# Scaling the gathered expert rows on ScalarE and adding them on VectorE eight tiles at a time

## The reference

```
out = x + attn(xn) + ffn(xn)
```

```
gates   = softmax(tokens @ Wg);  idx = argmax(gates);  kept = place < 1024
expert_out[e] = relu(expert_in[e] @ W1[e] + b1[e]) @ W2[e] + b2[e]
ffn[t]  = gates[t, idx] * kept * expert_out[idx][place of t]
```

## Time and profile before

| | us |
|---|---|
| median of three runs | 1358.07 (1357.27 to 1358.6) |
| the profiled execution: its span, from the first to the last instruction | 1358.0 |
| VectorE busy | 1248.0 (92%) |
| TensorE busy | 1012.7 (75%) |
| GpSimd busy | 930.7 (69%) |
| ScalarE busy | 749.5 (55%) |
| the 64 adds (L890), busy | 54.5 |
| the 64 gathers (L538), busy on GpSimd | 72.8 |

### The profile page before, as it was taken

The page is one execution under the profiler, slowest core; times in us unless marked ns, Lnnn a source line. Parts: engine busy times, 40 slices in busy tenths (PEclk is TensorE's granted clock), DMA queues, the critical chain, the costliest instruction groups (busy, mean ns, idle before and its releaser), DMA issues.

```text
span 1358.0 us, 15420 instructions
## 1 busy us (share of the span) xinstructions
PE 1012.7 (75%) x3725; PEld 468.5 (34%) x3725; DVE 1248.0 (92%) x1491; ACT 749.5 (55%) x1147; POOL 930.7 (69%) x737
## 2 busy tenths in 40 slices
PE   0867378888888888888788886776867677686675
PEld 0422134434344443434344442332322233232232
DVE  7689599898999979898999989999999999999997
ACT  2665247666566657666566655555555555555421
POOL 3248886677676757686677767686867768686655
PEclk9978579999899989999899999788988979898766
DMA  6512131211212121211212021111102121110211
GB/s 143 146 42 74 38 109 32 78 32 39 70 29 56 24 78 31 77 31 39 70 34 55 20 53 42 47 47 47 46 0 53 39 48 44 46 46 1 54 39 47
DMA packets 62895, 69.53 MB, mean 51 GB/s; under 512 B 11488, under 2 KB 49280, under 8 KB 62848
## 3 DMA queue, kind: packets, MB, share of 16 engines
q1 hardware_dynamic: 58752, 60.65, 18.0%
q0 software_dynamic: 4096, 8.40, 2.0%
HBM read 18.69 MB, written 16.78 MB: 26 GB/s over the span
## 4 chain that ended last, share of the span: by engine, by line
DVE 37%; issue 30%; PE 20%; POOL 5%; ACT 3%; SPq 2%; DVEq 2%; DMA 1%; POOLq 0%; ACTq 0%
DVE u_sb L899 14%; DVE s_sb L983 7%; PE bank L1185 3%; DVE sp_q L848 3%; POOL expert_in L567 3%; PE bank L1178 3%; PE bank L1203 3%; PE bank L1218 2%; DVE acc L890 2%; PE bank L1196 2%; PE bank L1144 2%; DVE g_sb L857 1%; PE bank L1161 1%; DVE dd L905 1%; DVE sp_l L851 1%
## 5 line engine op out<-in xcount | busy, mean ns | idle before, releaser
L560 POOL TENSOR_TENSOR s_sb<-s_sb,c_of 128x512 f32<-128x512 f32 x480 | 649.6, 1361 | 317.8 <-DVE s_sb L983 313.1
L983 DVE TENSOR_TENSOR_SCAN s_sb<-bank,u_sb 128x512 f32<-128x512 f32 x512 | 619.8, 1211 | 0.0
L739 ACT ACTIVATE bank<-bank,a_neg 128x510 f32<-128x510 f32 x512 | 337.2, 660 | 449.8 <-PE bank L1203 440.1
L1196 PE MATMUL bank<-dsp,sel_d 128*128 128x512 f32 x512 | 318.9, 623 | 102.0 <-DVE u_sb L899 91.0
L899 DVE TENSOR_TENSOR u_sb<-bank,b_of 128x512 f32<-128x512 f32 x512 | 345.4, 675 | 49.5 <-PE bank L1196 40.7
L1203 PE MATMUL bank<-dsp,sel_d 128*128 128x512 f32 x512 | 255.5, 499 | 117.0 <-DVE s_sb L983 110.4
L1196 PEld LDWEIGHTS bank<-dsp,sel_d 128*128 128x128 f32 x512 | 106.5, 208 | 305.4 <-DVE u_sb L899 238.5
L1203 PEld LDWEIGHTS bank<-dsp,sel_d 128*128 128x128 f32 x512 | 107.0, 209 | 262.9 <-DVE s_sb L983 241.7
L1218 PE MATMUL bank<-s_sb,con 128*32 128x512 f32 x1024 | 156.8, 688 | 28.1 <-POOL s_sb L560 24.2
L1129 PE MATMUL bank<-xnT,wx 128*128 (+1 forms) x256 | 133.1, 615 | 0.0
L567 POOL DMA_INDIRECT expert_in<-xn,put_at x64 | 68.1, 1065 | 22.2 <-issue 17.6
(11 more groups left out here) (134 smaller groups left out, 1117.2 us busy)
## 6 DMA issues: line engine op xcount, KB each, us to landing
dsp<-hi SPq DMA_DIRECT2D x64, 256.0 KB
dsp<-dd SPq DMA_DIRECT2D x64, 256.0 KB
expert_in<-dd SPq DMA_DIRECT2D x8, 512.0 KB, 6.2
xn<-expert_in SPq DMA_DIRECT2D x8, 512.0 KB, 4.2
xn<-L_ffn_W SPq DMA_DIRECT2D x16, 256.0 KB, 4.6
expert_out<-xn SPq DMA_DIRECT2D x16, 256.0 KB, 2.5
out<-acc SPq DMA_DIRECT2D x8, 512.0 KB, 5.2
expert_in<-xn,put_at POOLq DMA_INDIRECT x64, 2.2
```

The lines of the kernel that those rows point to most:

```text
L560: pool.tensor_tensor(s_now, s_now, c_of[:, hf, hh, :], ALU.mult).then_inc(S["p_ready"], 1)
L739: act.activation(d, d, ACT.Exp, scale=a_neg[:, k:k + 1]).then_inc(S["decay_ready"], 1)
L983: dve.tensor_tensor_scan(s_sb[:, w % S_RING, :], decay_of(w)[:, :], u_sb[:, w % U_RING, :], 0.0, ALU.mult, ALU.add).then_inc(S["scan_done" ...
L1196: pe.matmul(du_ps[w % 2][:, :], sel_d[:, group_of(w), :, :].rearrange("k n d -> k (n d)"), dsp[:, hf, head_of(w), 1, :], start=True, stop= ...
```

## The change

ScalarE multiplies the gathered rows by their gates, in place in `back`, one tile an instruction: two tiles in each of slots 10 to 13 (`SCALE` = 10, `SCALE_EACH` = 2), after the exponential of the slot and ahead of its other work. It waits for all eight gathers there. VectorE adds the whole group in one operation of 128x1024 in slot 16 and waits for the scaled tiles. The gates of a group are copied by VectorE to `gate_now`, next to the row numbers. For the last group, ScalarE scales all eight tiles after its last slot, and VectorE's add comes after the last gate and no longer before it.

```diff
-GATHER, COMBINE = 1, 14
+GATHER, SCALE, COMBINE = 1, 10, 16
+SCALE_EACH = 2
+        gate_now = sb("gate_now", [P, GROUP])
...
+            def scale_back(ch, tiles, extra=0):
+                act.wait_ge(S["back_loaded"], lin(ch, lambda c: 16 * GROUP * (c - FIRST_COMBINE + extra + 1)))
+                for n in tiles:
+                    act.activation(back[:, n, :], back[:, n, :], ACT.Copy, scale=gate_now[:, n:n + 1]
+                                   ).then_inc(S["back_scaled"], 1)
...
                     act.activation(d, d, ACT.Exp, scale=a_neg[:, k:k + 1]).then_inc(S["decay_ready"], 1)
+                    if has_combine(ch) and 0 <= w - SCALE < GROUP // SCALE_EACH:
+                        scale_back(ch, range((w - SCALE) * SCALE_EACH, (w - SCALE + 1) * SCALE_EACH))
...
-            chunks(act, body, lambda: None)
+            chunks(act, body, lambda: scale_back((CHUNKS - 1, None), range(GROUP), 1))
...
+                dve.tensor_copy(gate_now[:, :], gate[:, bass.ds(k, GROUP)])
                 dve.tensor_copy(take_now[:, :], take_at[:, bass.ds(k, GROUP)]).then_inc(S["take_ready"], 1)
...
-            def combine(ch, n, extra=0):
-                dve.wait_ge(S["back_loaded"], lin(ch, lambda c: 16 * GROUP * (c - FIRST_COMBINE + extra + 1)))
-                k = lin(ch, lambda c: (c - FIRST_COMBINE + extra) * GROUP + n)
-                rows = acc[:, bass.ds(k, 1), :].rearrange("p i d -> p (i d)")
-                return dve.scalar_tensor_tensor(rows, back[:, n, :], gate[:, bass.ds(k, 1)], rows,
-                                                ALU.mult, ALU.add)
+            def combine(ch, extra=0):
+                dve.wait_ge(S["back_scaled"], lin(ch, lambda c: GROUP * (c - FIRST_COMBINE + extra + 1)))
+                k = lin(ch, lambda c: (c - FIRST_COMBINE + extra) * GROUP)
+                rows = acc[:, bass.ds(k, GROUP), :]
+                return dve.tensor_tensor(rows, back[:, :, :], rows, ALU.add)
...
-                        if COMBINE <= w < COMBINE + GROUP:
-                            ins = combine(ch, w - COMBINE)
-                            if w == COMBINE + GROUP - 1:
-                                ins.then_inc(S["combined"], 1)
+                        if w == COMBINE:
+                            combine(ch).then_inc(S["combined"], 1)
...
-                for k in range(GROUP):
-                    ins = combine(end, k, 1)
-                ins.then_inc(S["combine_last"], 1)
                 gate_half(end, 1, 0)
                 gate_half(end, 1, 1)
+                combine(end, 1).then_inc(S["combine_last"], 1)
```

More of the change, by code:

```diff
@@ L201, in bass_mamba_moe @@
             "y_read g_ready misc_pe misc_act misc_dve misc_low misc_copy bc_hi sp_act sp_chain sp_done "
-            "delta_ready dx_ready dd_ready hi_ready lo_ready stacked ffn_loaded eo_free b1_ready take_ready back_loaded "
+            "delta_ready dx_ready dd_ready hi_ready lo_ready stacked ffn_loaded eo_free b1_ready take_ready back_loaded back_scaled "
             "combined combine_last out_stored act_chain in_w_loaded").split()}
@@ L1017, in body @@
                             take_indices(ch)
-                        if COMBINE <= w < COMBINE + GROUP:
-                            ins = combine(ch, w - COMBINE)
-                            if w == COMBINE + GROUP - 1:
-                                ins.then_inc(S["combined"], 1)
-                        if ch[0] == CHUNKS - 1 and w == min(COMBINE + GROUP, LAST_GATHER):
+                        if w == COMBINE:
+                            combine(ch).then_inc(S["combined"], 1)
+                        if ch[0] == CHUNKS - 1 and w == LAST_GATHER:
                             dve.wait_ge(S["combined"], TILES // GROUP - 1)
```

## The result

The changed kernel takes 1363.76 us, the median of four runs (1362.92 to 1365.22), against 1357.99 for the kernel before (four runs, 1357.27 to 1358.6). The ratio is 1.0044, with a 95% interval of 1.003 to 1.0058: slower by 4 to 8 us. The forecast was 1365.3.

The account below looks back on a forecast made before the run. VectorE was taken to bound the kernel, busy 1248.0 of 1358.0 us. Six chunks at +1.4 gave +8.4, chunk 15 -1.05, together +7.3: 1365.3 us, range 1353 to 1376.

Parts of the forecast that it names:

- part 1: VectorE's eight removed adds: worth 7.3 us of each loop chunk and 3.4 us in chunk 15.
- part 2: VectorE's added group add in slot 16: 2.25 us in chunks 9 to 14, 1.1 us in chunk 15.
- The scales: ScalarE's eight scales a chunk: 0.2 us of queue each, 1.6 us together, hidden after the first pair.
- part 4: ScalarE's moved wait for the gathers in slot 10: VectorE's B/C subtraction late, 5.8 us of stall a chunk.
- part 5: Denser slots 17 to 22 put GpSimd behind: the gate's multiply in slot 22 takes +0.59 us.
- part 6: VectorE's copy of the gates beside the index copy in slot 0: 0.06 us if before GpSimd's product.
- That rival, at +1.2: The gate copy in slot 0 waits for GpSimd: +1.2 us in each of six chunks, 1372.5 us; chance 0.11.
- the half-speed TensorE: Rival: TensorE leaves the stall slowly and VectorE waits 2 us in the chunk, 1377 us; chance 0.11.
- The sum: All terms of one chunk, 9 to 14, added: +1.4 us each, +8.4 us for six.
- the stall there: Chunk 15: the exponential of slot 11 ends at 1299.55, its scan 1.25 us late.
- the tail's 2.80 us: Time from a gather's issue to VectorE's release in the tail, 2.80 us, also used for chunk 15's last gather.

Follow-up runs that it names:

- add_17: The changed kernel with the group add in slot 17 in place of 16: 1359.87 us, ratio 1.0004.
- wait_only: The kernel before plus one instruction: ScalarE waits for all eight gathers in slot 10 and scales nothing; 1378.45 us, ratio 1.0146.
- late_scale: The changed kernel with ScalarE's scales in slots 14 and 15, four tiles each, and the group add in slot 17: 1324.8 us, ratio 0.9747.
- copy_first: The changed kernel with the scales and their wait at the end of ScalarE's slot, so slot 10's B/C copy goes first: 1358.56 us, ratio 0.9997.
- dve_two: The changed kernel without ScalarE's scales: VectorE multiplies the group by its gates in slot 15 and adds it in slot 17; 1340.09 us, ratio 0.9856.
- adds_in_one_slot: The kernel before with its eight small adds all in slot 17 in place of one in each of slots 14 to 21: 1334.53 us, ratio 0.9823.
- pool_add: late_scale with the group add of chunks 9 to 14 on GpSimd in slot 25: 1318.39 us, ratio 0.9696.

## Why the prediction was right

The sign, the size and the place were right, and most terms to a tenth of a microsecond. Per chunk, in order of the prediction's parts:

- The eight adds (part 1): VectorE's busy time fell by 4.6 us with the new group add in it, as 7.3 out and 2.25 and 0.6 in ask for.
- The group add (part 2): 2.25 forecast, 2.29 measured; add_17 showed the split, 1.2 of work and 1.1 of wait.
- The scales (part 3): 0.2 us of queue each forecast; two take 0.60 (904.99 to 905.59) and eight 2.44, so 0.3. A lone one takes 0.39 (at 1305.96, in chunk 15), and in a row 0.3. (The Trainium skill, "ScalarE: Activation LUTs", section "Rules for kernel authors": its budget gives 0.41 as an estimate, which agrees with the lone one.) The pair cost 0.2 us more than I counted.
- The premise of part 4 held: the last gather is issued 25.9 us after slot 0's copy (902.51 - 876.65), against 25.8 before, so it comes no earlier.
- The stall (part 4): 5.8 forecast, 5.74 measured, from two small errors that cancel: the gather was released 2.48 us after its issue and not 2.66, and the scales took 0.2 more. That it is ScalarE's wait, and no effect of the group add, wait_only and late_scale show from both sides; that its first victim was the B/C copy, and the exponential of slot 11 the next, copy_first.
- GpSimd's wait at the gate (part 5): +0.59 forecast, 1.22 - 0.66 = +0.56 measured.
- The gate copy (part 6): 0.06 forecast, 0.07 measured (876.65 to 876.72). That rival, at +1.2, did not come; for the second group, in slot 22 of chunk 15, the gates' copy does take 1.24 us, but there the index copy took 1.23 before. Nor did the half-speed TensorE cost time: over chunks 10 to 12 its granted clock was 0.81 to 0.87 in place of 0.85 to 0.89 and its busy time rose from 56.56 to 58.69 us, but VectorE's waits for it stayed at 7.1 us in six chunks. The prediction names for the lower clock; those rows do not show it.
- The sum: +1.4 forecast, 79.78 - 78.65 = +1.13 measured. The measured terms, with 0.08 off for the add's overlap, give 5.74 - 7.3 + 2.21 + 0.56 + 0.07 = +1.28. In chunk 10 VectorE's 32 multiplies and 33 scans were 5 and 3 ns shorter each than before, together 0.26 us, which no term holds.

Where it was off is chunk 15. I had -1.05 us; from its slot-0 copy to the end it takes 86.4 us (1362.0 - 1275.57) against 86.65 (1358.0 - 1271.35), so -0.2. The term at fault is the stall there: 1.25 forecast, 2.27 measured (VectorE's one wait for L748 above); with it the sum for chunk 15 would have been 0.0. I gave the last gather the tail's 2.80 us; it was issued at 1299.91 and released at 1303.64, after 3.73. In that stretch the DMA engines are busy, until 1302.8, mostly with the four transfers of 256 KB of the split `delta` (DMA busy tenths, 1299 to 1304 us, 40 slices):

```profile
DMA  9993995914999795958978999989830000000000
```

That the loads delayed the gather fits the row, and no run took them away, so it is argued and not shown. The trace of the kernel before had the same loads around its last gather, issued at 1295.67 (1290 to 1305 us, 40 slices; busy from 1293.0 to 1298.6):

```profile
DMA  0500000079989999997999400000000000000000
```

The two misses partly cancel, and that is luck: the loop came out 1.6 us under its forecast (6.8 in place of 8.4), chunk 15 0.9 us over.

The total by these terms is 6 x 1.13 - 0.2 = +6.6 us, within the measured 4 to 8. The two profiled spans differ by 4.0 only, because the changed kernel's profiled execution reached the stage 2.6 us earlier (slot-0 copy of the row numbers in chunk 9 at 796.87 and 799.44), in a part of the program that the change doesn't touch. The changed kernel's profiled execution took 1363.88 us in all, with a span of 1362.0: the 1.9 us around the span are counted in the times. The prediction took the span of before for the whole time, which didn't matter to a difference.

## What to carry to other kernels

A wait belongs on an engine only at the point where its lead over the consumers is longer than the wait; moved to an engine with half its time free but placed early in its queue, it stops whatever stands behind it, and cost 35 us here against the same work four slots later (add_17 and late_scale). Find the first instruction behind the wait that another engine needs, and the next, and price the queue that has built up by then too. For an operation that waits out another engine's instructions, count the meetings before the elements: of the eight adds' 7.9 us, some 5 were meetings.

## What the runs showed of the hardware

- VectorE can lose to GpSimd twice in a row: while GpSimd runs products back to back, a 1.2 us multiply that came just behind a scan took 2.88 us (median of dve_two's), and an add of 0.32 us took 2.28. With the products' mean of 1.24 us, both let one end of a product pass and ran only when GpSimd's series was over. At the gate of the earlier trace rows, with 1.25 us, it got in at the first end, and in late_scale an operation at 907.98, in a series of eight, took 0.67 us and waited for nothing. What tells the cases apart stays open. (The Trainium skill, "SBUF — State Buffer", section "SBUF: two separate sides", says that whichever starts first holds the pair for its whole instruction; that explains one product's wait and not the second.)
- The reverse holds as well: in adds_in_one_slot, two VectorE operations followed each other at 917.05 and 917.36 without a wait, while GpSimd's product, started at 917.20, took 1.96 us in place of 1.28.
- A gather of 128 rows of 512 bytes is usable by another engine 2.5 us after its issue when the DMA engines are idle, 2.8 in the tail, and 3.7 in the stretch with busy engines (one gather).
- A copy of 128x8 that takes 0.14 us took 1.23 in pool_add where GpSimd's product was running (slot 22 of chunk 15).
- The same 128x1024 add took 1.20 us on VectorE and 2.37 on GpSimd.
